# GNN edge sum on one core: full node ids in the rows, second-phase tiles that begin at any row, and a threshold product on 128 rows

## The reference

```python
edge_aggr = jnp.zeros((n, HIDDEN)).at[row].add(edge_features)      # row = src
combined = jnp.concatenate([x, edge_aggr, global_expand], axis=-1) @ W_c + b_c
h = softplus(combined @ W1 + b1)
h = softplus(h @ W2 + b2)
out = layernorm(x + h @ W3 + b3)
```

## Time and profile before

| what | us |
|---|---|
| median of three runs (2169.77 to 2183.89) | 2171.48 |
| the profiled execution, its own time | 2166.25 |
| its span in the trace | 2164.6 |
| first instruction of the first move until the last (L953) | 76.5 to 1630.4 |
| second phase on TensorE (L1019) | 1645.9 to 2078.5 |

### The profile page before, as it was taken

The page is one execution under the profiler, slowest core; times in us unless marked ns, Lnnn a source line. Parts: engine busy times, 40 slices in busy tenths (PEclk is TensorE's granted clock), DMA queues, the critical chain, the costliest instruction groups (busy, mean ns, idle before and its releaser), DMA issues.

```text
span 2164.6 us, 62457 instructions
## 1 busy us (share of the span) xinstructions
PE 1999.3 (92%) x15732; PEld 1762.3 (81%) x15732; DVE 1534.2 (71%) x5104; ACT 843.7 (39%) x2517; POOL 1163.2 (54%) x1351
## 2 busy tenths in 40 slices
PE   6408999999999999999999999999996999999975
PEld 3307888888888888888888888888886999999952
DVE  7505776777677777777776777777775888888857
ACT  0002222222222222222222222222224888888877
POOL 2205665665665566656655556565564555455424
PEclk9658999999999999999999999999997999999998
DMA  9975665666656566566665565665556999999932
GB/s 353 150 140 153 173 175 167 174 178 170 178 171 176 173 170 180 168 177 171 173 178 164 168 183 168 170 181 173 176 153 222 296 285 284 284 284 283 284 98 55
DMA packets 345473, 414.30 MB, mean 191 GB/s; under 512 B 28261, under 2 KB 249465, under 8 KB 344273
## 3 DMA queue, kind: packets, MB, share of 16 engines
q1 hardware_dynamic: 284579, 247.08, 39.4%
q0 software_dynamic: 53184, 163.38, 26.1%
q10 hardware_dynamic: 7689, 3.60, 0.8%
HBM read 233.69 MB, written 180.24 MB: 191 GB/s over the span
## 4 chain that ended last, share of the span: by engine, by line
PE 69%; POOLq 6%; issue 6%; POOL 6%; another core or an unknown queue 4%; ACT 3%; ACTq 2%; DMA 1%; DVE 1%; SPq 0%; DVEq 0%
PE ps L953 55%; PE ps L961 5%; POOL sums L454 5%; POOLq L449 4%; PE ps L1019 3%; PE ps L938 3%; PE ps L932 2%; ACTq L759 2%; PE ps L936 1%; POOLq L453 1%; ACT arena L827 1%; DMA buckets<-arena,index 1%; ACT arena L830 1%; ACT arena L828 1%
## 5 line engine op out<-in xcount | busy, mean ns | idle before, releaser
L953 PE MATMUL ps<-arena 128*120 128x129 f32 x9672 | 1286.8, 282 | 73.2 <-ACT arena L784 73.1
L429 POOL DMA_INDIRECT buckets<-arena,index x806 | 893.1, 1108 | 664.6 <-ACT arena L784 300.6
L953 PEld LDWEIGHTS ps<-arena 128*120 128x120 f32 x9672 | 1128.4, 184 | 99.1 <-issue 73.2
L784 ACT ACTIVATE arena<-ps 120x387 f32<-120x387 f32 x806 | 397.8, 494 | 1146.5 <-PE ps L953 734.2
L614 DVE TENSOR_SCALAR arena<-slot_no,slot_f 128x360 f32<-128x360 f16 x1612 | 586.2, 404 | 0.0
L1019 PE MATMUL ps<-mark,members 128*128 128x128 f32 x3648 | 426.3, 279 | 19.8 <-ACT mark L859 19.8
L1019 PEld LDWEIGHTS ps<-mark,members 128*128 128x128 f32 x3648 | 418.7, 193 | 27.3 <-issue 20.0
L682 DVE TENSOR_SCALAR mark<-node_no,members 128x128 f32<-128x128 f16 x1368 | 365.0, 328 | 71.8 <-DMA members<-buckets 46.1
L601 DVE TENSOR_TENSOR picked<-hotc,ps 128x392 f32<-128x392 f16 x202 | 113.5, 562 | 348.2 <-PE ps L938 344.0
L454 POOL TENSOR_TENSOR sums<-sums,staged 128x128 f32 x456 | 216.0, 474 | 227.0 <-ACT staged L847 206.3
L620 DVE TENSOR_SCALAR reach<-block_no,arena 50x120 bf16<-50x120 f16 x806 | 196.8, 244 | 0.0
(11 more groups left out here) (121 smaller groups left out, 578.8 us busy)
## 6 DMA issues: line engine op xcount, KB each, us to landing
members<-buckets SPq DMA_DIRECT2D x456, 258.0 KB, 3.4
arena<-in_feats SPq DMA_DIRECT2D x201, 512.0 KB
buckets<-arena,index POOLq DMA_INDIRECT x806
buckets<-sums SPq DMA_DIRECT2D x4, 3096.0 KB, 26.4
arena<-in_xT SPq DMA_DIRECT2D x12, 250.0 KB, 5.8
xn<-in_x ACTq DMA_DIRECT2D x1, 2800.0 KB
out_rows<-xn SPq DMA_DIRECT2D x12, 224.0 KB
buckets<-sums SPq DMA_DIRECT2D x1, 1032.0 KB, 39.1
```

What stands on the lines that cost most here:

```text
L429: pool.indirect_dma_start(units, bass.IndirectOffsetOnAxis(ap=index[0:SLOTS, s, b:b + 1], axis=0), rows[0:SLOTS, b, :], None).then_inc(sca ...
L784: act.activation(rows[0:SLOTS, b, :], ps[0:SLOTS, MOVED + b, 0:BLK], ACT.Copy).then_inc(rows_ready, 1)
L953: mm = pe.matmul(ps[0:SLOTS, MOVED + b, r * ROWF:(r + 1) * ROWF], perm[0:TP, b, t, r * SLOTS:(r + 1) * SLOTS], feat[0:TP, s, b * TPB + t, ...
```

## The change

- The node number in a row is the full id plus one; `local1` is made by one operation in place of two.
- A bucket begins right behind the one before it. The second phase's tiles begin at any row, and a bucket's last tile runs on over the rows of the next bucket: their ids match none of the tile's 128 nodes. So the 11 indirect and 5 static zero writes go; 4 indirect ones of 3 rows and one static one of 512 rows (behind the last bucket, ENDROW) stay.
- The row where a tile begins is computed (`tile_row`; ScalarE and VectorE, once) and SyncE loads it into a register for each step. The number of steps stays 456.
- VectorE subtracts a tile's first node from its four ids (`nodes`, one operation a step), two steps ahead of its marks; ScalarE takes its group from that result.
- `goto` and the threshold product of `rank` (L938) run on 128 rows: `reach`, `goto3`, `boff1_16` and `ident16` are used whole, with `border` and `boff1_16` cleared once by GpSimd.
- TensorE waits, before its first `rank`, for `window`, `first_node` and `past`, three copies that ScalarE makes from two small products.

```diff
-    SURE = -(-(E + K * STREAMS * GAP) // TROWS)
-    ZTILES = 12
-    DROWS = STEPS * TROWS + STREAMS * SPARE + ZEROS * ZROWS
+    ENDROW = E + K * STREAMS * GAP
+    DROWS = ENDROW + STREAMS * SPARE
...
             sp.wait_ge(zeros_set, 1)
-            for t in range(SURE, STEPS, ZTILES):
-                n = min(ZTILES, STEPS - t)
-                sp.dma_start(buckets[t * TROWS:(t + n) * TROWS, :].rearrange("(p r) f -> p (r f)", p=P),
-                             zero_src[:, 0:n * QR * ROWF]).then_inc(spare_zeroed, 16)
+            sp.dma_start(buckets[ENDROW:ENDROW + TROWS, :].rearrange("(p r) f -> p (r f)", p=P), zero_src[:, :])\
+              .then_inc(spare_zeroed, 16)
...
+            sp.wait_ge(tile_row_made, 1)
+
             def load_members(s, m):
+                row = sp.value_load(tile_row[0:1, bass.ds(s, 1)], min_val=0, max_val=ENDROW)
+                if not isinstance(s, int):
+                    sp.wait_ge(summed, s + (1 - MS))
                 sp.dma_start(members[:, m, :],
-                             buckets[bass.ds(s * TROWS, TROWS), :].rearrange("(p r) f -> p (r f)", r=QR))\
+                             buckets[bass.ds(row, TROWS), :].rearrange("(p r) f -> p (r f)", r=QR))\
                   .then_inc(members_loaded[m], 16)
...
             with sp.Fori(1, STEPS // MS) as i:
                 for m in range(MS):
-                    sp.wait_ge(summed, i * MS + (m + 1 - MS))
                     load_members(i * MS + m, m)
...
+            pool.memset(border[:, :], 0.0).then_inc(ones_set, 1)
+            pool.memset(boff1_16[:, :], 0.0).then_inc(ones_set, 1)
...
-            pool.wait_ge(spare_zeroed, 16 * -(-(STEPS - SURE) // ZTILES))
-            pool.wait_ge(zero_at_made, 2)
-            for z in range(ZEROS + STREAMS - 1):
-                n = (ZROWS if z < ZEROS else GAP) * ROWF
+            pool.wait_ge(zero_at_made, 1)
+            for o in range(STREAMS):
                 pool.indirect_dma_start(
-                    units, bass.IndirectOffsetOnAxis(ap=zero_at[0:K, z:z + 1], axis=0),
-                    zero_src[0:K, 0:n], None).then_inc(zeroed, 16)
-            pool.wait_ge(zeroed, 16 * (ZEROS + STREAMS - 1))
+                    units, bass.IndirectOffsetOnAxis(ap=zero_at[0:K, o:o + 1], axis=0),
+                    zero_src[0:K, 0:GAP * ROWF], None).then_inc(zeroed, 16)
+            pool.wait_ge(spare_zeroed, 16)
+            pool.wait_ge(zeroed, 16 * STREAMS)
...
-            dve.tensor_scalar(local1[0:TP, :], key16[0:TP, :], float(-P), 1.0, ALU.mult, ALU.add).then_inc(local_a, 1)
-            dve.wait_ge(local_a, 1)
-            dve.tensor_tensor(local1[0:TP, :], local1[0:TP, :], ids_i[0:TP, :], ALU.add).then_inc(local_a, 1)
+            dve.tensor_scalar(local1[0:TP, :], ids_i[0:TP, :], 1.0, None, ALU.add).then_inc(local_a, 1)
...
+            def tile_rows():
+                dve.wait_ge(past_copied, 1)
+                dve.scalar_tensor_tensor(past[0:1, :], tile_no[0:1, :], float(TROWS), past[0:1, :], ALU.mult, ALU.add)\
+                   .then_inc(tile_row_a, 1)
+                dve.wait_ge(tile_row_a, 1)
+                dve.tensor_scalar(tile_row[:, :], past[0:1, :], float(ENDROW), None, ALU.min).then_inc(tile_row_made, 1)
...
-                dve.tensor_scalar(reach[0:KS, b, 0:SLOTS], block_no[0:KS, 0:SLOTS], border[0:KS, bass.ds(g, 1)], None,
-                                  ALU.is_ge)\
+                dve.tensor_scalar(reach[:, b, 0:SLOTS], block_no[:, 0:SLOTS], border[:, bass.ds(g, 1)], None, ALU.is_ge)\
                    .then_inc(reach_made, 1)
...
+            def nodes(s, m, turn):
+                dve.wait_ge(members_loaded[m], turn * 16 + 16)
+                wait(dve, apart_made, s - 7)
+                dve.tensor_scalar(node_of[:, m, :], members[:, m, :].rearrange("p (r f) -> p r f", f=ROWF)[:, :, D],
+                                  first_node[:, bass.ds(s, 1)], None, ALU.subtract).then_inc(node_of_made, 1)
+
             def mark_nodes(s, m, turn):
-                dve.wait_ge(members_loaded[m], turn * 16 + 16)
+                if not isinstance(s, int) or s + 2 < STEPS:
+                    nodes(s + 2, (m + 2) % MS, turn + (m + 2) // MS)
+                dve.wait_ge(node_of_made, s + 1)
                 wait(dve, summed, s - 3)
                 for r in range(QR - 1):
-                    last = dve.tensor_scalar(mark[:, m % 4, r, :], node_no[:, :],
-                                             members[:, m, r * ROWF + D:(r + 1) * ROWF], None, ALU.is_equal)
+                    last = dve.tensor_scalar(mark[:, m % 4, r, :], node_no[:, :], node_of[:, m, r:r + 1], None,
+                                             ALU.is_equal)
...
+            act.wait_ge(window_done, 2)
+            act.activation(window[:, :], ps[0:1, WINDOW, 0:STEPS], ACT.Copy, scale=float(P)).then_inc(window_made, 1)
+            act.activation(first_node[:, :], ps[:, WINDOW, 0:STEPS], ACT.Copy, scale=float(P)).then_inc(window_made, 1)
+            act.activation(past[0:1, :], ps[0:1, PAST, 0:STEPS], ACT.Copy).then_inc(past_copied, 1)
...
-            pe.matmul(ps[0:KS, SMALL, 0:1], tri16[0:KS, 0:KS], small16[0:KS, 0:1], start=True, stop=True)\
+            pe.matmul(ps[0:KS, SMALL, 0:2], tri[0:KS, 0:KS], small[0:KS, 0:2], start=True, stop=True)\
...
-                    mm = pe.matmul(out_[:, b, :, :], boff1_16[0:K, bass.ds(c * CB + b, 1)].to_broadcast([K, TP]),
-                                   ident16[0:K, 0:K].unsqueeze(1).to_broadcast([K, TPB, K]), start=False,
+                    mm = pe.matmul(out_[:, b, :, :], boff1_16[:, bass.ds(c * CB + b, 1)].to_broadcast([P, TP]),
+                                   ident16[:, 0:K].unsqueeze(1).to_broadcast([P, TPB, K]), start=False,
...
-                pe.matmul(ps[0:SLOTS, GOTO + s % 2, b * 3:(b + 1) * 3], reach[0:KS, b, 0:SLOTS],
-                          goto3[0:KS, bass.ds(g, 1), :].rearrange("p g j -> p (g j)"), start=True, stop=True)\
+                pe.matmul(ps[0:SLOTS, GOTO + s % 2, b * 3:(b + 1) * 3], reach[:, b, 0:SLOTS],
+                          goto3[:, bass.ds(g, 1), :].rearrange("p g j -> p (g j)"), start=True, stop=True)\
                   .then_inc(reach_used, 1)
+            pe.wait_ge(window_made, 2)
+            pe.wait_ge(past_copied, 1)
             rank(0, 0)
```

More of the change, by code:

```diff
@@ L227, in gnn_bucketed_edge_sum_mlp_layernorm @@
         goto_a = sem("goto_a")
[L228 removed]
+        ends_made = sem("ends_made")
+        past_copied = sem("past_copied")
+        tile_row_a = sem("tile_row_a")
+        tile_row_made = sem("tile_row_made")
         window_done = sem("window_done")
@@ L540, in _ @@
                .then_inc(tiles_a, 1)
+            dve.tensor_copy(small[0:KS, 0:1], incl_f[0:KS, JB - 1:JB]).then_inc(tiles_made, 1)
             dve.wait_ge(tiles_a, 1)
@@ L919, in _ @@
                   .then_inc(rise_done, 1)
-            pe.wait_ge(starts_made, 1)
-            pe.matmul(ps[0:1, WINDOW, 0:STEPS], ones16[0:KS, 0:1], starts16[0:KS, :], start=True, stop=True)\
+            pe.wait_ge(ends_made, 2)
+            pe.matmul(ps[:, WINDOW, 0:STEPS], ones16[0:K, :], ends16[0:K, :], start=True, stop=True)\
+              .then_inc(window_done, 1)
+            pe.wait_ge(counts_a, 1)
+            pe.matmul(ps[0:1, PAST, 0:STEPS], small16[0:K, 0:1], ends16[0:K, :], start=True, stop=True)\
               .then_inc(window_done, 1)
```

95 lines of the change are left out of this document (48 added, 47 removed).

## The result

The changed kernel takes 2204.14 us (median of 4, 2196.15 to 2212.35) beside 2171.5 for the kernel before (4 runs, 2169.77 to 2183.89): a ratio of 1.0138, interval 1.0084 to 1.0192. It is slower by 1.4%, where 2079 and a gain of 4% had been predicted. The profiled execution took 2201.54 us, its span is 2199.8.

The account below looks back on a forecast made before the run. TensorE was taken to bound both phases, after a 73 us standstill at the start, with SyncE close behind in the second. -82 - 160 + 150 = -92 gave 2079 us for the median; own range 2040 to 2125, wide range 1990 to 2220.

Parts of the forecast that it names:

- rival A: Weight loads in phase one: 128 rows free none, while SyncE's new load sets phase two's pace; 2229 us, chance 0.18.
- rival C: Phase two: the register load takes 600 ns on SyncE, +290 instead of +150; 2219 us, chance 0.06.
- Part 1: Start of the kernel: most zero writes go, so TensorE no longer stands still behind them; -82 us.
- the slow clock behind the stop: Start: three batches after TensorE's standstill took 9.9 us against 5.6 at the steady pace; losing that saves 4.3 us.
- part 2: First phase: with `goto` and `rank` products on 128 rows, weight loads come forward; 1.82 to 1.62 us a batch, -160 us.
- I take 1.62, for others come near: First phase: 1.62 us a batch instead of TensorE's own 1.575, because GpSimd, VectorE and ScalarE are close behind.
- Part 3: Second phase: SyncE's register load per step lengthens its step to 1.23 to 1.26 us and sets the pace; +150 us.
- rival B: Second phase: SyncE's load is cheap and VectorE takes over at 1.0 us a step, +47; 1976 us, chance 0.14.
- Part 4: Rest of the second phase: `nodes`, ScalarE's group, reads beginning at any row and empty tiles cost 0.
- near 1375: Sign that the forecast is right: the first phase is over near 1375 us.
- Rival D: First phase: the scatter's landing takes over at about 1.72 us a batch, part 2 is -80; 2159 us, chance 0.08.

Follow-up runs that it names:

- group 2: Runs beside which the kernel before took about 2150 to 2154 us (second, third and fifth series, three chips); the unchanged changed kernel took 2021.99 and 2031.19 us there.
- group 1: Runs beside which the kernel before took about 2171 to 2175 us (two series on one chip; the predicted pair is put here by its time); changed kernel 2204.14 us.
- fifth series: Runs on group 2, kernel before 2153.57 us: changed kernel unchanged, 2031.19 us (ratio 0.942); with three idle sequencer instructions inside each move, 2039.5 us.

## Why the prediction was wrong

The forecast was 2079 with a ratio of 0.957; the pair measured 1.0138. The time lies within the wide range (1990 to 2220), which says little: it is outside the forecast's own 2040 to 2125, in the part that belonged to rivals A and C, and it came about by another mechanism than theirs.

*Part 1, zero writes, -82:* right in mechanism and nearly in size. The ninth batch starts 82.3 us earlier, where the sum gives 77.5 for it (73.3 + 4.7 - 0.5): 4.6 before the first move, 73.1 of standstill, and 4.6 because the first eight batches ran closer, which the sum didn't have. The 4.3 for the slow clock behind the stop come on top; they lie in the stretch counted under part 2 here.

*Part 2, products on 128 rows, -160:* this is the step that failed. Its mechanism was right: the loads are brought forward, and move to move is 1.43 us where 1.45 was worked out. By the Trainium skill ("TensorE: Matmul & The Clock Gate", Part 3, What overlaps and what doesn't) a load on the same rows as the running product would not overlap; the trace disagrees here, as it did at the earlier trace rows, with `goto`'s load of 128 rows starting 0.27 us before the end of the move. So rival A's ground is refuted. What was mis-sized is the term "I take 1.62, for others come near": 1.790 was measured in the pair, so that -34 came in place of -160, well under the 68 at which, by its own sum, the change stops paying. Of the 0.17 between, 0.12 is TensorE standing still; the rest isn't accounted for. Beside it stand TensorE's late signals, up to 4.7 us late for SyncE in the changed kernel. That they are what costs the time follows from the comparison with group 2, where the same kernel has punctual signals and 1.571 a batch; no run on group 1 has the 128 rows with punctual signals. I had bounded the pace by the busy time of each engine, and none of those terms was wrong; that the hand-over itself may take microseconds wasn't in the sum. Nor could the trace before have given its size, for the lateness grew with the change. SyncE's issues over 0.5 us late are 9% in the kernel before, 16% with the full change on 50 rows, 53% in the kernel before on 128 rows and 71% in the changed kernel, all on group 1. On group 2 the changed kernel has none over 0.20 us. It takes both the products on 128 rows and a chip of group 1.

*On chips where the signals are in time,* part 2 is bigger than predicted. With parts 1 and 3 as measured the changed kernel would take 2153.7 - 82 + 151 = 2223 with the old products on group 2; it takes 2022: -201, or 0.25 a batch, at 1.571 (the bound given was -196, at 1.575). The fifth series gives -191 in the same way (2031). This difference is worked out; the kernel with 50 rows wasn't run on group 2. That the old products run near 1.6 a batch there too is ruled out by the kernel before, which has them and gains only some 20 us on group 2.

*Part 3, SyncE's register load, +150:* right, +151.3 at 1.24 us a step (predicted 1.23 to 1.26), with SyncE setting the pace. Its composition is a little different: some 118 fall to the register load, and about 35 remain without it, at 1.03 to 1.05 a step. That is rival B's state, which was put at 1.0 a step and +47. The step came out longer and the price smaller, for the "0.90 us a step" of before is 0.93 by the prediction's own row (1718 products, eight a step, in 200 us) and 0.95 over the whole phase. `nodes` was put at 0.1 to 0.2 us and takes 0.25. The load took 267 ns, near the 288 of the earlier trace rows and far from rival C's 600.

*Part 4, nothing for reads that begin at any row and for `nodes`:* right while SyncE's step covers them. Loads land in 3.0 us, 3.4 before. Without that cover the prediction had 25 us; the run without the register load shows 35.

One of its signs doesn't follow from its own sum: the first phase over "near 1375" should read 1630 - 82 - 160 = 1388. Nothing else hangs on it.

*Rival D* named the place (TensorE idle behind ScalarE in the first phase) and a part 2 of half the size (2159 in all), but not the cause: eight row buffers bring nothing on group 1, and on group 2 ScalarE waits 604 us for landings at full pace.

*What stays open:* why TensorE's signals are late on group 1. The ends of products in the trace are modelled, so that the exact lateness of one signal is uncertain by what the model errs; the bunched updates show that signals are late, and on group 2 the same model fits within 0.04 us. The kernel that breaks up TensorE's stream of products met only group 2. Nor is it known whether group 1 is more than one chip, or that the chip itself, and not something else that the series of group 1 share, makes the difference.

## What to carry to other kernels

The busy times of the engines bound a pace only if the signals between them come at once. Look in the trace at how late the waiting engines start after an instruction has ended, before an edit and after it; here the edit itself made the lateness common, so keep a range for it ahead of the run. When experiments are spread over chips, run the unchanged kernels, before and changed, beside them on each; three edits in a row looked like the cure here, and the kernel without them was nearly as fast beside them. And a register load in the loop of a DMA queue costs its whole chain of small instructions (SyncE's step went from 0.6 us to 1.24), not the 0.27 of the load alone: fetch many values with one, and drop the bounds test where the values are already clamped.

## What the runs showed of the hardware

- The same two kernels stand at 1.014 (1.0084 to 1.0192) on one chip and at 0.942 (0.9396 to 0.9445) on another, while the kernel before differs by only 1% between them (2171.5 and 2153.57). The median duration of the move's products is 273 ns on both, and the granted clock is 1.00 in these stretches on both. What differs is when a signal of TensorE's comes.
- On group 1 a signal of TensorE's came 2.54 us after its product's end, and the next two followed 0.16 and 0.17 us behind it, though their products are 1.43 us apart. The waiting engines started 0.02 to 0.03 us after the signal.
- Weight loads of 128-row bf16 products are brought forward between float32 products of 128 rows: a `goto` of three columns costs 1.43 less 1.344, about 0.09 us, where on 50 rows it cost 0.316.
- A register load on SyncE takes 267 ns for one value and 529 ns for eight.
